# Indirect transfers of a two-layer graph kernel, issued with and without a bound on their indices

## The chip, the cores and the metric

One core of a Trainium2 chip runs the whole kernel. The metric is the device time of one execution in microseconds (us); lower is better. The kernel before was timed three times.

## What is computed

The reference has 8192 nodes with 128 features each and a dense 0/1 adjacency matrix `adj` of 8192 x 8192 with few ones in a row. Two layers, cut to what matters:

```
h = relu(layernorm(x));  H = h @ W.T + b;  s = H @ a_s;  r = H @ a_r
e = leaky_relu(adj * s + adj * r.T);  att = softmax(where(adj > 0, e, -9e15), axis=1)
x = x + att @ H                                     # layer 0
h = relu(layernorm(x)) @ weight
out = relu(adj @ h + bias)
x = x + max over the neighbours j of row i of out[j]   # layer 1
```

## The kernel before, in words

The kernel never multiplies by the whole matrix where it need not. It first turns each row of `adj` into a list of the numbers of its neighbours: tiles of 128 rows stream in by SP's queue, TensorE packs 8 columns into a word (line 862), VectorE finds the words that are not zero with MAX8 (lines 1115 to 1124) and takes them apart. Rows are ordered by their degree, so that the 128 rows of a ranked tile have lists of about one length. There are 63 ranked tiles in four groups (`SLOTS`: 523 list columns in all), and the 128 heaviest rows, the hubs, apart.

GpSimd (POOL) moves everything by those lists. Its program, in order:

- Lines 530 to 540: the table `h_table` (row 0 is a neutral row, row n + 1 is node n) is written from SBUF, 16 direct transfers.
- `rank_group(g)`, four times: each tile of records is scattered to its ranked place (line 547), with direct loads of the next group (525, 527) and of the ranked lists (552).
- `gather_h(q)` (line 563), 63 tiles, 523 transfers: for each list column j one indirect transfer fetches 128 rows of `h_table`, one for each partition, into a slot of `ring`. `ring` has 64 slots; a gather waits on `s_att` until VectorE has used a slot. After each gather, `scatter_y` of the tile five places back (line 576) writes 128 rows of layer 0's result to `y_table`.
- `gather_y(m)` (line 600), 177 transfers, with `scatter_p` (line 608): the sum over neighbours for the light half of the rows. At the same time TensorE multiplies the heavy half by dense bits (line 1010).
- `gather_p(n)` (line 638), 66 tiles, 662 transfers (554 by `srec`, 108 by `seg_slots` for the hubs), with `store_out` (line 645): the maximum over neighbours. VectorE reduces each tile with a tree (line 1225, waits for the gather), adds the input (line 1444), and in between does the rounds that list the hubs' neighbours (lines 1399 to 1412).

A missing neighbour has index 0, the neutral row. No index is beyond its table. The kernel before gives each indirect transfer `bounds_check`, the largest index that may occur. The three gathers also say `oob_is_err=False` (a row with a larger index would be skipped); the four scatters leave that argument at its default, `True`.

```
ring[:, A_AT[q] + j, :], None, h_table,
bass.IndirectOffsetOnAxis(srec_u[g][:, i, LIST + j:LIST + j + 1], 0),
bounds_check=N, oob_is_err=False).then_inc(s_rows[q % BUFS], 16)
```

Counted in the code: 63 + 523 + 63 + 177 + 32 + 662 + 63 = 1583 indirect transfers, all issued by GpSimd.

Of the kernel before, what the change touches and what calls it, by code (L numbers as in the profile page):

```python
# [9 lines left out]
P = 128  # L10
N = 8192
D = 128
# [31 lines left out]
S, RS, OWN, OFF, LEN, ROW, ROW1, OWN1, LIST = range(9)  # L44
# [14 lines left out]
BUFS = 4  # L59
RECORDS = 8  # L60
RESULTS = 8
# [3 lines left out]
def ring_plan(slots, size):  # L65

    first, at = [], 0
    for k in slots:
        if at % size + k > size:
            at += size - at % size  # L70
        first.append(at)
        at += k
    return [a % size for a in first], [sum(b < a + k - size for b in first) for a, k in zip(first, slots)]
# [26 lines left out]
C_AT, C_LEFT = ring_plan(C_SLOTS, RING)  # L100
# [22 lines left out]
def segment_tile(n):  # L123

    return n - HUB_AT if HUB_AT <= n < HUB_AT + HUB_TILES else None


def ranked_tile(n):

    return n if n < HUB_AT else n - HUB_TILES  # L130
# [13 lines left out]
def build(nc, x, adj, W0, b0, a_s, a_r, W1, b1, out):  # L144
    ctx = ExitStack()
    with ctx:
        def sb(name, shape, dt=F32):
            return ctx.enter_context(nc.sbuf_tensor(name, shape, dt))
# [4 lines left out]
        def sem(name):  # L153
            return ctx.enter_context(nc.semaphore(name))
# [3 lines left out]
        p_table = nc.dram_tensor("p_table", [N + 1, D], F32).ap()  # L158
# [11 lines left out]
        ring = sb("ring", [P, RING, D + 1])  # L170
# [8 lines left out]
        rec = [rec_all[:, g % 2, 0:n * (LISTS + LIST + w)].rearrange("p (n c) -> p n c", n=n)  # L179
               for g, (_, n, w) in enumerate(GROUPS)]  # L180
        rec_u = [r.bitcast(U32) for r in rec]
        srec = [sb(f"srec{g}", [P, n, LIST + w]) for g, (_, n, w) in enumerate(GROUPS)]
        srec_u = [r[:].bitcast(U32) for r in srec]
        trec = sb("trec", [P, RECORDS, LISTS])
        results = sb("results", [P, RESULTS, D])
        y_save = rec_all[:, 0, 0:(NR - DENSE_FROM) * D].rearrange("p (m d) -> p m d", d=D)
# [132 lines left out]
        s_onehot, s_counted, s_ranked, s_rec = (sem(n) for n in ("s_onehot", "s_counted", "s_ranked", "s_rec"))  # L319
        s_recin, s_srec = sem("s_recin"), sem("s_srec")  # L320
        s_rows = [sem(f"s_rows{i}") for i in range(BUFS)]
# [5 lines left out]
        s_result = [sem(f"s_result{i}") for i in range(RESULTS)]  # L327
# [3 lines left out]
        s_pscat = [sem(f"s_pscat{i}") for i in range(BUFS)]  # L331
# [174 lines left out]
        def _(pool):  # L506
# [16 lines left out]
            def load_rows(g):  # L523
                a, n, _ = GROUPS[g]
                pool.dma_start(rec[g][:, :, 0:D], x[a * P:(a + n) * P, :].rearrange(
                    "(t p) c -> p t c", p=P)).then_inc(s_recin, 16)
                pool.dma_start(rec[g][:, :, D:LISTS], h_table[a * P + 1:(a + n) * P + 1, :].rearrange(
                    "(t p) c -> p t c", p=P)).then_inc(s_recin, 16)
# [13 lines left out]
            def rank_group(g):  # L542
                _, n, w = GROUPS[g]
                pool.wait_ge(s_recin, 32 * (g + 1))
                pool.wait_ge(s_ranked, g + 1)
                for i in range(n):
                    pool.indirect_dma_start(records[g], bass.IndirectOffsetOnAxis(rank[:, g, i:i + 1], 0),  # L547
                                            rec[g][:, i, :], None, bounds_check=n * P - 1).then_inc(s_rec, 16)
                if g < 3:
                    load_rows(g + 1)  # L550
                pool.wait_ge(s_rec, 16 * sum(m for _, m, _ in GROUPS[:g + 1]))
                pool.dma_start(srec[g][:], records[g][:, LISTS:].rearrange("(t p) c -> p t c", p=P)).then_inc(
                    s_srec, 16)
                pool.wait_ge(s_srec, 16 * (g + 1))

            def gather_h(q):
                g, i, k = RANKED[q]
                if A_LEFT[q] > 0:
                    pool.wait_ge(s_att, A_LEFT[q])
                if q >= BUFS:  # L560
                    pool.wait_ge(s_att, q - BUFS + 1)
                for j in range(k):
                    pool.indirect_dma_start(  # L563
                        ring[:, A_AT[q] + j, :], None, h_table,
                        bass.IndirectOffsetOnAxis(srec_u[g][:, i, LIST + j:LIST + j + 1], 0),
                        bounds_check=N, oob_is_err=False).then_inc(s_rows[q % BUFS], 16)

            def y_row(q):
                return results[:, q % RESULTS, :] if q < DENSE_FROM else y_save[:, q - DENSE_FROM, :]

            def scatter_y(q):
                g, i, _ = RANKED[q]
                pool.wait_ge(s_copied, TURNS[STEP[q] + 3] + 1)
                if q >= RESULTS:
                    pool.wait_ge(s_result[q % RESULTS], 16 * (q // RESULTS))
                pool.indirect_dma_start(y_table, bass.IndirectOffsetOnAxis(srec_u[g][:, i, ROW1:ROW1 + 1], 0),
                                        y_row(q), None, bounds_check=N).then_inc(s_result[q % RESULTS], 16)

            for q in range(NR):
                if RANKED[q][1] == 0:  # L580
                    rank_group(RANKED[q][0])
                gather_h(q)
                if q >= LAG:
                    scatter_y(q - LAG)
            for q in range(NR - LAG, NR):
                scatter_y(q)
# [6 lines left out]
            def gather_y(m):  # L593
                g, i, k = RANKED[DENSE_FROM + m]
                if Y_LEFT[m] > 0:
                    pool.wait_ge(s_ysum, Y_LEFT[m])
                if m >= BUFS:
                    pool.wait_ge(s_ysum, m - BUFS + 1)
                for j in range(k):
                    pool.indirect_dma_start(  # L600
                        ring[:, Y_AT[m] + j, 0:D], None, y_table,
                        bass.IndirectOffsetOnAxis(srec_u[g][:, i, LIST + j:LIST + j + 1], 0),
                        bounds_check=N, oob_is_err=False).then_inc(s_rows[m % BUFS], 16)

            def scatter_p(m):
                g, i, _ = RANKED[DENSE_FROM + m]
                pool.wait_ge(s_ysum, m + 1)
                pool.indirect_dma_start(p_table, bass.IndirectOffsetOnAxis(srec_u[g][:, i, ROW1:ROW1 + 1], 0),  # L608
                                        y_save[:, m, :], None, bounds_check=N).then_inc(s_pscat[m % BUFS], 16)

            for m in range(len(Y_SLOTS)):
                gather_y(m)
                if m >= 3:
                    scatter_p(m - 3)
            for m in range(len(Y_SLOTS) - 3, len(Y_SLOTS)):
                scatter_p(m)
# [7 lines left out]
            def gather_p(n):  # L624
                k = C_SLOTS[n]
                if C_LEFT[n] > 0:
                    pool.wait_ge(s_max, C_LEFT[n])
                if n >= BUFS:
                    pool.wait_ge(s_max, n - BUFS + 1)
                for j in range(k):  # L630
                    if segment_tile(n) is not None:
                        slot = seg_slots[:, segment_tile(n), j:j + 1]
                    else:
                        q = ranked_tile(n)
                        g, i, _ = RANKED[q]
                        column = LIST + j if j < A_SLOTS[q] else OWN1
                        slot = srec_u[g][:, i, column:column + 1]
                    pool.indirect_dma_start(  # L638
                        ring[:, C_AT[n] + j, 0:D], None, p_table, bass.IndirectOffsetOnAxis(slot, 0),
                        bounds_check=N, oob_is_err=False).then_inc(s_rows[n % BUFS], 16)  # L640

            def store_out(n):
                g, i, _ = RANKED[ranked_tile(n)]
                pool.wait_ge(s_max, n + 1)
                pool.indirect_dma_start(out, bass.IndirectOffsetOnAxis(srec_u[g][:, i, ROW:ROW + 1], 0),  # L645
                                        results[:, n % RESULTS, :], None, bounds_check=N - 1).then_inc(
                                            s_result[n % RESULTS], 16)

            for n in range(NC):
                if n == HUB_AT:  # L650
                    pool.wait_ge(s_segin, 16)
                gather_p(n)
                if n >= 3 and segment_tile(n - 3) is None:
                    store_out(n - 3)
            for n in range(NC - 3, NC):
                store_out(n)
# [872 lines left out]
```

## Time and profile before

| | |
|---|---|
| median of 3 runs | 3168.51 us (3162.12 to 3172.34) |
| the profiled execution, its own time | 3148.13 us |
| its span | 3146.3 us |
| POOL busy | 1666.1 us (53%), 1628 instructions |
| VectorE busy | 1667.3 us (53%) |
| TensorE busy | 921.0 us (29%) |
| indirect transfers, line 638, p_table by srec | 567.4 us in 554 |
| indirect transfers, line 563, h_table | 547.5 us in 523 |

A POOL row of a transfer is the time in which GpSimd makes its descriptors, not the time in which the bytes move. POOLq is GpSimd's sequencer: register moves and waits stand under it and are not counted as busy. "Idle before" is the engine's gap before an instruction, with what ended it; "issue" there means that nothing in the profile was waited for.

### The profile page before, as it was taken

What the parts mean: (1) busy time and instruction counts of PE and PEld (TensorE: products, weight loads), DVE (VectorE), ACT (ScalarE), POOL (GpSimd) and SP (SyncE); (2) the same over time, 40 slices, a digit from 0 to 9 for tenths busy, and PEclk for the clock granted to TensorE, in tenths of its full rate; (3) what the DMA queues carried; (4) which work ended last, traced back from release to release, by engine and by line L of the source; (5) the groups of instructions that cost most, each with busy time, mean ns of one, the idle gap of its engine ahead of it and who ended that gap; (6) DMA issues with size and microseconds to landing.
All of it is one profiled execution on the core that took longest, in us unless ns stands there. A gap on an engine that the chain in (4) does not pass through costs nothing.

```text
span 3146.3 us, 19516 instructions
## 1 busy us (share of the span) xinstructions
PE 921.0 (29%) x3633; PEld 419.3 (13%) x3633; DVE 1667.3 (53%) x4416; ACT 377.8 (12%) x769; POOL 1666.1 (53%) x1628
## 2 busy tenths in 40 slices
PE   4785232334323440130017969900000000000000
PEld 1442111111101110120003424400000000000000
DVE  6658878888565686553462535446961431102111
ACT  2331012222000123342330000000000000000000
POOL 0011522333556656755655564366536777667676
PEclk8667666676666775565558979955555555555555
DMA  9679866578857875353222222151203111222121
GB/s 357 234 267 421 248 246 237 208 282 304 253 224 282 314 272 158 67 140 73 72 72 49 69 49 60 39 122 51 58 24 41 49 52 48 46 47 51 43 49 45
DMA packets 121044, 450.31 MB, mean 143 GB/s; under 512 B 31666, under 2 KB 69636, under 8 KB 112596
## 3 DMA queue, kind: packets, MB, share of 16 engines
q1 hardware_dynamic: 42676, 304.96, 24.8%
q0 software_dynamic: 55488, 123.23, 17.3%
q10 hardware_dynamic: 22752, 20.82, 2.1%
q14 instruction: 97, 0.79, 0.1%
q8 instruction: 31, 0.51, 0.1%
HBM read 409.76 MB, written 39.12 MB: 143 GB/s over the span
## 4 chain that ended last, share of the span: by engine, by line
DVE 23%; issue 21%; POOL 17%; PE 16%; DVEq 13%; POOLq 4%; DMA 3%; ACT 2%; SPq 1%; ACTq 0%
POOL ring L638 14%; PE psV L1010 11%; DVE ring L1225 3%; POOLq L638 3%; DVE a_buf L1399 2%; DVE words L1124 2%; DVE words L1115 2%; DVE words L1119 2%; DVEq L1123 2%; DVEq L1118 2%; DVEq L1403 2%; PE psV L862 2%; DVEq L1237 2%; DVE found L1148 1%; DVEq L1147 1%
## 5 line engine op out<-in xcount | busy, mean ns | idle before, releaser
L563 POOL DMA_INDIRECT ring<-h_table,srec x523 | 547.5, 1047 | 501.8 <-DVEq L1247 289.1
L638 POOL DMA_INDIRECT ring<-p_table,srec x554 | 567.4, 1024 | 228.9 <-issue 179.3
L1225 DVE TENSOR_TENSOR ring<-ring 128x128 f32<-128x128 f32 (+8 forms) x498 | 239.7, 481 | 667.9 <-DMA ring<-p_table,srec 465.9
L862 PE MATMUL psV<-a_buf,bit_ident 128*128 128x512 bf16 x1024 | 350.4, 514 | 253.4 <-DVE V L1117 156.7
L1010 PE MATMUL psV<-rec_all,a_buf 128*128 128x512 bf16 x1008 | 236.1, 387 | 37.6 <-issue 36.9
L600 POOL DMA_INDIRECT ring<-y_table,srec x177 | 179.9, 1016 | 56.1 <-issue 55.8
L1020 PE MATMUL psH<-ones_row,flag_col 128*1 128x1 f32 x2 | 0.2, 163 | 691.8 <-DVEq L1470 691.8
L862 PEld LDWEIGHTS psV<-a_buf,bit_ident 128*128 128x128 bf16 x1024 | 122.3, 123 | 471.2 <-issue 227.2
L923 PE MATMUL psT<-ident,hn 128*128 128x128 f32 x63 | 27.4, 438 | 516.4 <-ACT hn L734 450.3
L1375 DVE TENSOR_SCALAR rec_all<-a_buf 128x512 uint16<-128x512 uint16 x336 | 77.4, 302 | 124.7 <-remote 69.9
L638 POOL DMA_INDIRECT ring<-p_table,seg_slots x108 | 108.0, 1000 | 47.8 <-issue 32.3
L1010 PE MATMUL psV<-wbuf,a_buf 128*128 128x512 bf16 x528 | 123.2, 390 | 30.0 <-DVE wbuf L1375 22.4
L532 POOL DMA_DIRECT2D h_table<-stage x16 | 12.3, 767 | 211.9 <-ACT rs_col L689 211.9
L1010 PEld LDWEIGHTS psV<-rec_all,a_buf 128*128 128x128 bf16 x1008 | 97.8, 97 | 169.4 <-issue 53.8
L1115 DVE MAX8 words<-psV 128x8 f32<-128x1024 f32 x63 | 77.7, 1233 | 50.3 <-PE psV L871 32.7
L645 POOL DMA_INDIRECT out<-results,srec x63 | 66.4, 1054 | 70.5 <-DVEq L1445 44.8
L547 POOL DMA_INDIRECT records<-rec_all,rank x63 | 63.2, 1003 | 72.4 <-DVEq L1201 53.5
L608 POOL DMA_INDIRECT p_table<-rec_all,srec x32 | 33.8, 1057 | 121.7 <-DVEq L1364 116.6
L1020 PEld LDWEIGHTS psH<-ones_row,flag_col 128*1 128x1 f32 x2 | 0.1, 80 | 692.0 <-issue 692.0
L1124 DVE MAX8 words<-V 128x8 f32<-128x1024 f32 x65 | 79.8, 1228 | 9.9 <-issue 5.5
L1399 DVE MAX8 a_buf<-V 128x8 f32<-128x1024 f32 x60 | 73.7, 1228 | 20.8 <-issue 16.8
L923 PEld LDWEIGHTS psT<-ident,hn 128*128 128x128 f32 x63 | 11.7, 186 | 535.5 <-issue 532.9
(221 smaller groups left out, 2095.1 us busy)
## 6 DMA issues: line engine op xcount, KB each, us to landing
a_buf<-in_adj SPq DMA_DIRECT2D x64, 4096.0 KB
ring<-p_table,srec POOLq DMA_INDIRECT x554
ring<-h_table,srec POOLq DMA_INDIRECT x523
packed<-wbuf ACTq DMA_DIRECT2D x32, 256.0 KB
a_buf<-packed SPq DMA_DIRECT2D x8, 1024.0 KB
trec<-records ACTq DMA_DIRECT2D x63, 128.5 KB
h_table<-stage POOLq DMA_DIRECT2D x16, 258.0 KB, 6.1
a_buf<-r_row SPq DMA_DIRECT2D x1, 4096.0 KB
```

The lines of the kernel that those rows point to most:

```text
L547: pool.indirect_dma_start(records[g], bass.IndirectOffsetOnAxis(rank[:, g, i:i + 1], 0), rec[g][:, i, :], None, bounds_check=n * P - 1).th ...
L563: pool.indirect_dma_start(ring[:, A_AT[q] + j, :], None, h_table, bass.IndirectOffsetOnAxis(srec_u[g][:, i, LIST + j:LIST + j + 1], 0), bo ...
L600: pool.indirect_dma_start(ring[:, Y_AT[m] + j, 0:D], None, y_table, bass.IndirectOffsetOnAxis(srec_u[g][:, i, LIST + j:LIST + j + 1], 0), ...
L638: pool.indirect_dma_start(ring[:, C_AT[n] + j, 0:D], None, p_table, bass.IndirectOffsetOnAxis(slot, 0), bounds_check=N, oob_is_err=False). ...
L645: pool.indirect_dma_start(out, bass.IndirectOffsetOnAxis(srec_u[g][:, i, ROW:ROW + 1], 0), results[:, n % RESULTS, :], None, bounds_check= ...
L862: last = pe.matmul(psV[n % 2][:, h * BANK:(h + 1) * BANK].rearrange("p (g n) -> p g n", n=P), bit_ident[:, k, :], rows[:, :, k, :], start= ...
L1010: last = pe.matmul(psA[c % 2], y_part[i][:, at:at + D], bit_rows[(c * BLOCKS + b) % 3][:, k, :], start=(b == 0 and k == 0 and i == 0), sto ...
L1115: dve.max(words[:, 0:8], src)
L1124: dve.max(words[:, r:r + 8], V[:])
L1225: dve.tensor_tensor(ring[:, at:at + h, 0:D], ring[:, at:at + h, 0:D], ring[:, at + n - h:at + n, 0:D], op)
L1375: last = dve.tensor_scalar(bit_rows[n % 3][:, k, :].bitcast(U16).rearrange("p (u n) -> p u n", n=P), words_in[c % 2][:, :, b * P:(b + 1) * ...
L1399: dve.max(best, V[:])
```

## The change

All seven kinds of indirect transfer lose their `bounds_check`, and the three gathers lose `oob_is_err=False` with it. The sizes, the order of the instructions, the semaphores and the tables stay.

```diff
                     pool.indirect_dma_start(records[g], bass.IndirectOffsetOnAxis(rank[:, g, i:i + 1], 0),
-                                            rec[g][:, i, :], None, bounds_check=n * P - 1).then_inc(s_rec, 16)
+                                            rec[g][:, i, :], None).then_inc(s_rec, 16)
...
                     pool.indirect_dma_start(
                         ring[:, A_AT[q] + j, :], None, h_table,
-                        bass.IndirectOffsetOnAxis(srec_u[g][:, i, LIST + j:LIST + j + 1], 0),
-                        bounds_check=N, oob_is_err=False).then_inc(s_rows[q % BUFS], 16)
+                        bass.IndirectOffsetOnAxis(srec_u[g][:, i, LIST + j:LIST + j + 1], 0)).then_inc(s_rows[q % BUFS], 16)
...
                 pool.indirect_dma_start(y_table, bass.IndirectOffsetOnAxis(srec_u[g][:, i, ROW1:ROW1 + 1], 0),
-                                        y_row(q), None, bounds_check=N).then_inc(s_result[q % RESULTS], 16)
+                                        y_row(q), None).then_inc(s_result[q % RESULTS], 16)
```

Lines 600 and 638 change as line 563 does, lines 608 and 645 as line 576 does.

In the built program a bound is held in a register. So before the change each of the 1583 indirect transfers has a register move ahead of it on GpSimd (1586 moves in all), and the transfer names that register; after it, 3 moves are left and the transfers name none. Where the kernel waits for a semaphore right before such a transfer, the last wait is carried by the move before the change, and by the transfer itself after it. Nothing moves on the other engines.

## Rows read from the trace of the kernel before

**Rows 1.** The page, busy tenths in 40 slices of the span
```profile
DVE  6658878888565686553462535446961431102111
...
POOL 0011522333556656755655564366536777667676
```

**Rows 2.** Busy time by stretch; columns are named in the first row
```profile
core 0: us, PE busy (x) PEld busy (x) DVE busy (x) ACT busy (x) POOL busy (x), PEclk, DMA share, GB/s
230.00:800.00 570.00, 214.56 (x787) 85.19 (x785) 478.54 (x1187) 103.22 (x166) 190.20 (x187) 0.68 0.76 281
800.00:1205.00 405.00, 133.64 (x420) 50.39 (x420) 265.80 (x725) 51.70 (x95) 236.23 (x223) 0.67 0.70 253
1205.00:1645.00 440.00, 64.81 (x305) 51.32 (x305) 232.60 (x692) 142.12 (x302) 278.17 (x264) 0.53 0.38 99
1645.00:2054.00 409.00, 355.91 (x1568) 154.03 (x1568) 177.31 (x693) 9.61 (x16) 205.45 (x201) 0.91 0.21 55
2054.00:2310.00 256.00, 0.00 (x0) 0.00 (x0) 180.74 (x248) 0.00 (x0) 155.34 (x151) 0.50 0.27 69
2310.00:3147.00 837.00, 0.19 (x2) 0.11 (x2) 187.76 (x410) 0.00 (x0) 585.55 (x574) 0.50 0.22 46
```

**Rows 3.** Waits of POOL from 2310 us to the end: total, times, longest
```profile
POOL ring L638 <- DVEq L1445: 60.2, 7, 26.8
```

**Rows 4.** Waits of VectorE, whole span: total, times, longest
```profile
DVE ring L1225 <- DMA ring<-p_table,srec: 465.9, 46, 61.9
```

**Rows 5.** POOL in order of time, two places: start, duration, gap before (none: no bracket)
```profile
321.25 1.25 POOL L527 DMA_DIRECT2D rec_all<-h_table  x1
...
2613.84 1.00 POOL L638 DMA_INDIRECT ring<-p_table,srec  x1 [0.30 <-issue]
2615.14 1.00 POOL L638 DMA_INDIRECT ring<-p_table,srec  x1 [0.30 <-issue]
2616.45 1.04 POOL L645 DMA_INDIRECT out<-results,srec  x1 [0.31 <-issue]
```

**Rows 6.** Line 563 from 351 to 361 us: count, ns min/median/max, starts
```profile
L563 POOLq MOVE  x19: 29/29/29, 351.2 to 360.5; - x19
L563 POOL DMA_INDIRECT ring<-h_table,srec x7: 997/997/1070, 351.9 to 359.9; - x7
```

**Rows 7.** The lines of the transfers, whole span: ns min/median/max of one
```profile
L638 POOL DMA_INDIRECT ring<-p_table,srec x554: 991/997/2623, 2053.2 to 3130.6; - x185
...
L547 POOL DMA_INDIRECT records<-rec_all,rank x63: 973/976/1599, 299.0 to 1458.2; - x63
...
L645 POOL DMA_INDIRECT out<-results,srec x63: 978/1039/1390, 2128.5 to 3136.2; - x63
...
L532 POOL DMA_DIRECT2D h_table<-stage x16: 750/750/981, 80.5 to 227.3; - x16
...
L527 POOL DMA_DIRECT2D rec_all<-h_table x4: 1153/1214/1255, 234.9 to 1230.2; - x4
```

**Rows 8.** Chain of waits, then all engines in order of time, 547 and 203 us
```profile
547.57 0.03 DVEq L1247
...
548.45 1.02 POOL L563 DMA_INDIRECT ring<-h_table,srec  x1 [11.85 <-DVEq L1247]
...
203.54 0.20 ACT L689 ACTIVATE rs_col<-psH 128x4 f32<-128x4 f32 x1
204.03 0.75 POOL L532 DMA_DIRECT2D h_table<-stage  x1 [11.04 <-ACT rs_col L689]
```

**Rows 9.** Waits of POOL on VectorE, 800 to 1205 us, then 1205 to 1645 us
```profile
POOL ring L563 <- DVEq L1247: 102.9, 9, 45.0
...
POOL y_table L576 <- ACT rec_all L748: 42.4, 8, 10.7
POOL y_table L576 <- DVEq L1247: 13.8, 4, 5.6
```

More of the change, by code:

```diff
@@ L601, in gather_y @@
                         ring[:, Y_AT[m] + j, 0:D], None, y_table,
-                        bass.IndirectOffsetOnAxis(srec_u[g][:, i, LIST + j:LIST + j + 1], 0),
-                        bounds_check=N, oob_is_err=False).then_inc(s_rows[m % BUFS], 16)
+                        bass.IndirectOffsetOnAxis(srec_u[g][:, i, LIST + j:LIST + j + 1], 0)).then_inc(s_rows[m % BUFS], 16)
             def scatter_p(m):
@@ L608, in scatter_p @@
                 pool.indirect_dma_start(p_table, bass.IndirectOffsetOnAxis(srec_u[g][:, i, ROW1:ROW1 + 1], 0),
-                                        y_save[:, m, :], None, bounds_check=N).then_inc(s_pscat[m % BUFS], 16)
+                                        y_save[:, m, :], None).then_inc(s_pscat[m % BUFS], 16)
             for m in range(len(Y_SLOTS)):
@@ L638, in gather_p @@
                     pool.indirect_dma_start(
-                        ring[:, C_AT[n] + j, 0:D], None, p_table, bass.IndirectOffsetOnAxis(slot, 0),
-                        bounds_check=N, oob_is_err=False).then_inc(s_rows[n % BUFS], 16)
+                        ring[:, C_AT[n] + j, 0:D], None, p_table, bass.IndirectOffsetOnAxis(slot, 0)).then_inc(s_rows[n % BUFS], 16)
             def store_out(n):
@@ L645, in store_out @@
                 pool.indirect_dma_start(out, bass.IndirectOffsetOnAxis(srec_u[g][:, i, ROW:ROW + 1], 0),
-                                        results[:, n % RESULTS, :], None, bounds_check=N - 1).then_inc(
+                                        results[:, n % RESULTS, :], None).then_inc(
                                             s_result[n % RESULTS], 16)
```

## The prediction

> **What bounds the kernel now.** I read the page's slices first, to see which engine is dense in which stage [rows 1]: VectorE leads in the first third, and in the last third only POOL has work all the time, at 6 or 7 tenths. Six or seven tenths do not look like a bound, so the second look is at the gaps. POOL in order of time [rows 5] shows one shape over and over: an indirect transfer of 1.00 us, 0.30 us of nothing, the next one, a period of 1.30 us. The gap is "issue": nothing is waited for. So POOL is full when busy time plus 0.305 us for each transfer fills the stretch. By stretches [rows 2]:
>
> - 2310 us to the end: 585.6 + 574 x 0.305 = 761 us of 837. POOL's waits for VectorE are 60.2 us more [rows 3]; that is nearly all of it. VectorE has 188 us of work and waits for the gathers, 465.9 us over all of line 1225 [rows 4]. So this stretch is as long as POOL's 574 transfers and those waits.
> - 1205 to 1645 us: 278.2 + 264 x 0.305 = 359 of 440, 0.81.
> - 800 to 1205 us: 236.2 + 223 x 0.305 = 304 of 405, 0.75. Here VectorE still takes the adjacency apart and POOL waits for it, 102.9 us in 9 waits [rows 9].
> - 230 to 800 us: VectorE busy 478.5 of 570, POOL 190. 1645 to 2054 us: TensorE busy 355.9 of 409. 2054 to 2310 us: VectorE busy 180.7 of 256 and its drains. In these three POOL has slack.
>
> What a nanosecond less per transfer is worth: all 574 of the last stretch less the part behind waits (60 of 837, so 0.93), 534; of the 264, 0.8, 211; of the 223, where POOL and VectorE wait for each other by turns, I take half, 112. Together some 850 transfers. The rest, 187 + 201 + 151, are covered by VectorE, TensorE and VectorE; the tightest is the last of them, where POOL's transfers and gaps fill 155.3 + 151 x 0.305 = 201 us of 256, so they could be a quarter dearer before that cover goes.
>
> **The change, part by part.**
>
> 1. *The register moves.* 1583 x 29 ns [rows 6] would be 46 us if they stood in POOL's way. They do not. Between 351.2 and 360.5 us the sequencer did 19 moves, with the transfers between them, so one turn of move and transfer is 9.3 / 18 = 0.52 us, while POOL got through 7 transfers [rows 6]. The sequencer runs ahead until its queue is full and is then paced by POOL's 1.30 us. Taking 29 ns off a turn of 0.52 us beneath one of 1.30 us gives 0. What hides it is POOL's own work; the cover goes only if a transfer costs POOL under 0.52 us.
>
> 2. *The 0.305 us gap.* It is the same before gathers and scatters, and a direct transfer that follows another has none (line 527 stands right behind 525) [rows 5]. Since the sequencer is ahead, the move is not in it. I cost the gap at no change. Bounds: 0.305 us less if it were made by the bound (850 x 0.305 = 259 us less), nothing more. I take 0, because rows 6 shows that the sequencer isn't late.
>
> 3. *The work of one transfer.* No row shows an unbounded indirect transfer. From below: a direct transfer of 512 rows takes 750 ns, one of 2048 rows 1214 ns, so a row costs 0.3 ns and the gather's 997 ns for 128 rows [rows 7] hold 247 ns or more that direct ones lack: fetching the indices, turning them into addresses, and the check. If all of that were the check: 850 x 0.247 = 210 us less. From above: scatters behind gathers, whose bound is of the default kind, take 1039 ns, 42 more than a gather [rows 7]. If that were the kind of the bound, and an unbounded gather behaved like them, 850 x 0.042 = 36 us more. The nearest row is the scatter of records, line 547: indirect, 128 rows, one after the other with none of another sort between, and without the skipping of rows: 976 ns, 21 less than a gather. I take 21 ns: skipping, which only the gathers have, needs a decision for each row, and the unbounded gather makes none. About 0.93 of the transfers are gathers: 850 x 0.93 x 0.021 = 17 us less.
>
> 4. *The waits.* Before, the last wait sits on the move; when it ends, the transfer behind is still to be decoded and handed over. VectorE's drain on line 1247, which releases the gather, ends at 547.60, and POOL starts at 548.45 [rows 8]: 0.85 us. Where the transfer itself waits, a direct one, ACT ends at 203.74 and POOL starts at 204.03 [rows 8]: 0.29 us. The 0.305 us of an indirect transfer remain to it, so I expect about 0.60 us after the change, 0.25 less; between none and 0.56 less. This counts only for a wait at which POOL really stood and only where POOL is on the path: 7 in the last stretch [rows 3], 9 + 8 + 4 between 800 and 1645 [rows 9], of which I take half: 18 x 0.25 = 5 us less, 0 to 10.
> The Trainium skill ("Perfetto Trace Analysis", section DMA Instruction — SWDGE (GPSIMD)) says that such an instruction is decoded, put into a wait queue with its semaphore wait, and that the sequencer then goes on; by that a wait on the transfer hides its decoding. The 0.29 us of the direct transfer agree.
>
> 5. *Bytes and order.* The same rows move; a faster POOL brings the gathers 2% closer together against a DMA share of 0.22 [rows 2]. Nothing.
>
> Sum: 17 + 5 = 22 us less. The profiled execution took 3148.1 us, so 3126 us in a profile like it; the three timed runs had their median at 3168.5, 20 us above, so 3146 us there. I forecast that median. From about 10 us on, 0.3%, a measurement of this kernel can tell a change from none; spread over 850 transfers that is 11 ns each, which is little, and so the sign hangs on a small cost.
>
> **The rivals.**
>
> *A. The check costs nothing that POOL feels* (chance 0.33). It may run on all rows at once, or on a path that is taken anyway with a bound that is never met. For: 997 against 976 may come from gather against scatter and not from skipping; a row of a direct transfer costs only 0.3 ns, so rows are handled many at a time. Then only the waits are left: 5 us less, 3163, within 0.3%.
> The Trainium skill ("DMA: Bandwidth & Descriptors", section Anatomy of one DMA) calls descriptor generation "small, variable", with most of a transfer's fixed cost in its completion; by that page this rival would hold. The trace disagrees for this kernel as to the whole, since POOL's 1.30 us per transfer set the last stretch, but as to the check it shows nothing.
>
> *B. The check is most of what is special about indirect transfers* (chance 0.10). Then up to 247 ns each, half of it 850 x 0.12 = 105 us less, 3064; all of it, 2958. Against: 128 comparisons are little beside fetching 128 indices from as many partitions.
>
> *C. The unbounded gather is dearer* (chance 0.15). With `oob_is_err=False` the gathers leave a mode of their own and join that of the scatters. Place: line 638 after 2310 us. Price: up to 42 ns, 36 us, less 5 for the waits, 31 more: 3199. It decides from 17 ns per gather on (11 for the bound of a measurement and 6 to pay for the waits). For: the 1039 ns. Against: line 547, of the same mode, has 976 ns, so the 1039 look like the cost of changing from gather to scatter, which line 645 does each time.
>
> *D. The bound is still applied*, from the size of the table. The built program names no bound, so I count this with A.
>
> **How the numbers follow.** My forecast, 10 to 60 ns less for a gather (8 to 47 us, with the waits 13 to 52), has 0.42; A 0.33; B 0.10; C 0.15. Faster by over 0.3%: 0.42 + 0.10 - 0.02 for its lower edge = 0.50. Within: A and the lower edges of the forecast and of C, 0.38. Slower: 0.12. The range leaves out B's greater half with a bit of its lesser, and the upper half of C: 3085 to 3182.
>
> **What would show it.** In the profile after: the row of the sequencer's moves on lines 563 and 638 is gone and the 0.30 us gap stays (if it shrinks, step 2 is wrong); the median of line 638 is about 976 (997 would be A, under 900 B, over 1015 C); line 547, which never skipped, stays at 976; after a wait, POOL starts about 0.60 us behind the drain (0.85 would refute step 4); the last stretch is some 15 us shorter, and 1645 to 2054 us is as long as now. The whole argument fails if the stretches before 2054 us get longer although POOL's transfers do not, which I have no row for.

## The result, and the profile after

| | kernel before | the change |
|---|---|---|
| median | 3163.0 us (3155.4 to 3176.0, 10 runs) | 3179.1 us (3172.2 to 3183.7, 10 runs) |
| ratio | | 1.0033, 95% interval 1.0017 to 1.0048 |
| the profiled execution, its own time | 3148.1 us | 3180.2 us |
| its span | 3146.3 us | 3170.0 us |

Slower by 16 us between the medians and by some 10 us by the ratio (0.0033 x 3163), where 22 us faster was forecast. The time is inside the range, the sign is not. Of the two profiled executions the one of before is 15 us under its median and the one of the change is on it, so some 15 us of what stands between the two traces are no work of the change.

From line 566 on the change's own lines are one to three lower than before: 563 gathers for layer 0 as before, 575 scatters y, 599 gathers y, 636 gathers for the last stage, 642 scatters the output; VectorE's 1247 is 1244, its 1445 is 1442.

By line, whole span, ns min/median/max of one, beside [rows 7]:

```profile
L563 POOL DMA_INDIRECT ring<-h_table,srec x523: 938/944/2802, 352.0 to 1634.9; - x175
L636 POOL DMA_INDIRECT ring<-p_table,srec x554: 940/944/2868, 2089.1 to 3147.2; - x185
L547 POOL DMA_INDIRECT records<-rec_all,rank x63: 956/960/1597, 299.6 to 1486.3; - x63
L642 POOL DMA_INDIRECT out<-results,srec x63: 974/987/1889, 2160.5 to 3152.8; - x63
```

Of the 1586 register moves 3 are left. A gather has fallen from 997 to 944 ns, the scatter of the output from 1039 to 987, the scatter of records from 976 to 960. So a transfer costs POOL less than forecast, and the kernel is slower. POOL in order of time in the change shows the gap unchanged:

```profile
559.37 0.94 POOL L563 DMA_INDIRECT ring<-h_table,srec  x1 [0.30 <-issue]
560.62 0.94 POOL L563 DMA_INDIRECT ring<-h_table,srec  x1 [0.30 <-issue]
```

Busy time by stretch in the change, columns as in [rows 2]:

```profile
800.00:1205.00 405.00, 138.51 (x414) 50.87 (x421) 245.39 (x654) 39.72 (x74) 208.46 (x215) 0.66 0.72 256
1645.00:2054.00 409.00, 325.24 (x1406) 143.23 (x1436) 187.96 (x702) 11.10 (x24) 206.91 (x214) 0.87 0.23 58
2310.00:3170.00 860.00, 0.19 (x2) 0.11 (x2) 220.72 (x460) 0.00 (x0) 591.62 (x586) 0.50 0.22 46
```

From 800 to 1205 us VectorE gets through 654 instructions where it got through 725 [rows 2], and POOL through 215 transfers where it was 223. The work there has not grown, it is late. The best ruler for that is the start of the n-th transfer on POOL, since both programs issue the same 1612 in the same order (us from the start of the span, from the two traces):

| transfer | where it stands | before | the change | later by |
|---|---|---|---|---|
| 71 | a gather of layer 0, first group | 394.1 | 392.5 | -1.6 |
| 271 | a gather of layer 0, second group | 932.7 | 937.5 | 4.8 |
| 421 | a scatter of y, near the end of the second group | 1195.7 | 1227.9 | 32.2 |
| 921 | a gather, 34th transfer of the last stage | 2099.2 | 2132.2 | 33.0 |
| 1611 | the last but one | 3134.8 | 3151.4 | 16.6 |
| 1612 | the last | 3136.2 | 3152.8 | 16.6 |

The last stage gives 16 us back, as forecast, and what stands behind it takes nearly all of them away again. POOL's closing drain, first of before, then of the change (ns, start):

```profile
L146 POOLq DRAIN  x1: 7114/7114/7114, 3138.9 to 3138.9; - x1
```

```profile
L146 POOLq DRAIN  x1: 17700/17700/17700, 3152.1 to 3152.1; - x1
```

From the start of the last transfer to the end of the execution it is 12 us before (3136.2 to 3148.1) and 27 us in the change (3152.8 to 3180.2). Of the 15 us more, 7 lie inside the span and 8 outside it: the execution is 1.8 us longer than its span before, and 10.1 to 11.2 us in all ten executions of the change. What the drain waits for is not shown: the last packet of a transfer's data starts at 3155.1 us, 14.7 us before the drain ends. Taken off the two medians, the last transfer would start at some 3151 us before and 3152 us in the change (an estimate, since each kernel's end is read in one profile). At the medians, then, what is lost early and what is won in the last stage about cancel, and the 16 us are those at the end.

Up to 32 us (part of them the good luck of the profile of before) are lost ahead of transfer 421, where POOL stands at waits for VectorE. Waits of POOL from 380 to 1205 us, first of before, then of the change (total, times, longest):

```profile
POOL ring L563 <- DVEq L1247: 277.9, 19, 67.1
```

```profile
POOL ring L563 <- DVEq L1244: 319.2, 17, 76.6
```

41 us more. And VectorE, which POOL waits for, is idle for nothing. Its waits from 800 to 1205 us that the profile puts down to "issue", in the change:

```profile
DVE rec_all L1175 <- issue: 10.5, 1, 10.5
DVE found L1140 <- issue: 10.4, 6, 3.1
DVE found L1145 <- issue: 10.2, 7, 2.5
DVE node L1137 <- issue: 9.9, 6, 2.5
DVE e_sc L1212 <- issue: 9.2, 3, 3.8
```

and in the kernel before:

```profile
DVE node L1140 <- issue: 9.7, 5, 2.5
DVE l_inv L1235 <- issue: 8.9, 3, 4.2
DVE found L1148 <- issue: 8.9, 6, 2.4
DVE found L1143 <- issue: 8.8, 5, 2.4
DVE rec_all L1178 <- issue: 7.0, 1, 7.0
```

The profile finds nothing that these instructions wait for; most of them read what VectorE itself has just written. Over all lines the "issue" time of VectorE in this stretch is 103.7 us before and 130.5 us in the change. I call them **stalls**. They were in the trace that I predicted from, and I had no term for them. Where VectorE stalls many times in a row, in the change around 390 us, its starts lie 1.40 and 2.81 us apart, multiples of 0.70:

```profile
385.71 0.49 DVE L1130 TENSOR_TENSOR node<-words_no,bit_node 128x320 f32<-128x320 int32 x1 [2.02 <-issue]
387.11 0.49 DVE L1134 SCALAR_TENSOR_TENSOR node<-bits,node 128x320 f32<-128x320 int32 x1 [0.91 <-issue]
...
389.92 0.57 DVE L1137 SCALAR_TENSOR_TENSOR node<-node,label 128x320 f32<-128x320 f32 x1 [2.31 <-issue]
```

POOL has them too, late in the kernel. The chain of waits, kernel before, around 2700 us:

```profile
2699.84 0.70 POOLq L638
2700.53 0.45 POOL ring L638
2700.99 0.25 issue
2701.24 0.70 POOLq L638
```

The register move, 29 ns elsewhere [rows 6], takes 0.70 us here: 286 of GpSimd's moves and waits do, all of them after 2586 us. In the change there are none, but from about 2896 us on more than half of its transfers fall into a beat of 1.40 us, twice 0.70, where they could come every 1.25:

```profile
2904.98 1.10 POOL L636 DMA_INDIRECT ring<-p_table,srec  x1 [0.30 <-issue]
2906.38 1.09 POOL L636 DMA_INDIRECT ring<-p_table,srec  x1 [0.30 <-issue]
2907.77 1.10 POOL L636 DMA_INDIRECT ring<-p_table,srec  x1 [0.30 <-issue]
```

### The profile page after: what moved, and what is told of

Read it like the earlier page. It is cut to its first block, busy times and chain, and to the rows that moved or that the text cites. A ratio compares the mean times of both kernels' runs of the same rounds, so it can differ in the third digit from the quotient of the medians.

```text
span 3170.0 us, 17872 instructions
## 1 busy us (share of the span) xinstructions
PE 919.7 (29%) x3572; PEld 423.6 (13%) x3633; DVE 1666.1 (53%) x4416; ACT 377.8 (12%) x769; POOL 1605.9 (51%) x1628
## 4 chain that ended last, share of the span: by engine, by line
DVE 22%; POOL 22%; issue 20%; PE 16%; DVEq 13%; DMA 3%; ACT 2%; SPq 1%; another core or an unknown queue 1%; ACTq 0%; POOLq 0%
POOL ring L636 17%; PE psV L1007 11%; DVE ring L1222 3%; POOL ring L563 2%; DVE a_buf L1396 2%; DVE words L1121 2%; DVE words L1112 2%; DVE words L1116 2%; DVEq L1120 2%; DVEq L1115 2%; DVEq L1400 2%; PE psV L859 2%; DVEq L1234 2%; POOL out L642 1%; DVE found L1145 1%
## 5 line engine op out<-in xcount | busy, mean ns | idle before, releaser
L563 POOL DMA_INDIRECT ring<-h_table,srec x523 | 517.1, 989 | 556.3 <-DVEq L1244 346.9
L636 POOL DMA_INDIRECT ring<-p_table,srec x554 | 554.7, 1001 | 216.9 <-issue 171.2
L599 POOL DMA_INDIRECT ring<-y_table,srec x177 | 171.1, 967 | 56.0 <-issue 56.0
L1372 DVE TENSOR_SCALAR wbuf<-a_buf 128x512 uint16<-128x512 uint16 x176 | 40.0, 300 | 110.2 <-remote 64.3
L1396 DVE MAX8 a_buf<-V 128x8 f32<-128x1024 f32 x60 | 73.7, 1228 | 23.9 <-issue 20.0
L1121 DVE MAX8 words<-V 128x8 f32<-128x1024 f32 x65 | 79.8, 1228 | 8.4 <-issue 3.9
```

The costliest lines, as they stand in the source:

```text
L563: pool.indirect_dma_start(ring[:, A_AT[q] + j, :], None, h_table, bass.IndirectOffsetOnAxis(srec_u[g][:, i, LIST + j:LIST + j + 1], 0)).th ...
L599: pool.indirect_dma_start(ring[:, Y_AT[m] + j, 0:D], None, y_table, bass.IndirectOffsetOnAxis(srec_u[g][:, i, LIST + j:LIST + j + 1], 0)). ...
L636: pool.indirect_dma_start(ring[:, C_AT[n] + j, 0:D], None, p_table, bass.IndirectOffsetOnAxis(slot, 0)).then_inc(s_rows[n % BUFS], 16)
L1121: dve.max(words[:, r:r + 8], V[:])
L1372: last = dve.tensor_scalar(bit_rows[n % 3][:, k, :].bitcast(U16).rearrange("p (u n) -> p u n", n=P), words_in[c % 2][:, :, b * P:(b + 1) * ...
L1396: dve.max(best, V[:])
```

## The experiments

### Taking the change apart, on a chip with stalls

The change does two things: a transfer is cheaper, and no move stands ahead of it, so that waits sit on the transfer. Two theories stood: P, the cheaper transfers do the harm, by what their denser stream does to VectorE; W, the wait on the transfer does it. Four kernels, run on one chip beside the kernel before (3173.4 us there, 13 runs).

**reg_once** has the moves gone and the transfers as before: all bounds stay, but the values (n x 128 - 1, N, N - 1) are put into registers once.

```diff
+            bound = {v: held(pool, v) for v in sorted({n * P - 1 for _, n, _ in GROUPS} | {N, N - 1})}
...
-                        bounds_check=N, oob_is_err=False).then_inc(s_rows[q % BUFS], 16)
+                        bounds_check=bound[N], oob_is_err=False).then_inc(s_rows[q % BUFS], 16)
```

> All bounds are kept, but each of the four values is put in a register once, so no register move stands ahead of a transfer and the waits sit on the transfers, as after the change. Theory W (the changed kernel's loss between 930 and 1130 us comes with the instruction stream: no moves, waits on the transfers): this kernel shows that loss too, about 30 us more in that stretch, with transfers of 997 ns, so 3185 to 3210 us. Theory P (the loss comes because cheaper transfers shift the gathers against VectorE's steps): gathers of 997 ns, no loss in that stretch, 3155 to 3170 us.

**nop_wait** has the cheap transfers alone: no bounds, and a no-op of the sequencer that carries the wait, where the move stood.

```diff
+                    ahead(pool)
                     pool.indirect_dma_start(
```

> No bounds, but a no-operation of the sequencer stands ahead of each indirect transfer and carries its wait, where the register move stood before. Theory W: gathers of 944 ns and no loss between 930 and 1130 us, so the change's saving shows: 3163 less about 35, 3125 to 3140 us. Theory P: the loss stays, 3170 to 3185 us.

**first_only** takes the bounds from lines 547, 563 and 576 alone, **last_only** from lines 638 and 645 alone (the diff is that of the change, cut to these lines).

> Only the transfers of layer 0 (lines 547, 563, 576) lose their bounds. Both theories: the loss of some 30 us before 1205 us shows here and nothing is won after it, 3180 to 3195 us. If the loss is chance of single executions, 3150 to 3165 us.

> Only the transfers of the last stage (lines 638, 645) lose their bounds. Until 2054 us as before; then 574 transfers at 53 ns less are 30 us less, of which the changed kernel's last 250 us, where the transfers came at 1.40 us each, may take back some 15: 3133 to 3150 us under both theories. If the last stage wins nothing, 3160 us and more.

| | ratio to before | 95% interval | transfer 421 at | transfers 921 to 1611 | last transfer to the end | VectorE's stalls, whole span |
|---|---|---|---|---|---|---|
| before | | | 1195.7 us | 1035.6 us | 12 us | 168 us |
| reg_once (moves gone) | 0.992 | 0.9901 to 0.9939 | 1206.1 | 1022.5 | 21 | 172 |
| last_only | 0.9956 | 0.9939 to 0.9973 | 1208.0 | 1019.4 | 27 | 177 |
| nop_wait (cheap transfers) | 1.007 | 1.0052 to 1.0087 | 1234.4 | 1040.2 | 12 | 213 |
| first_only | 1.0035 | 1.0019 to 1.0052 | 1238.4 | 1037.2 | 12 | 202 |
| the change (both) | 1.0033 | 1.0017 to 1.0048 | 1227.9 | 1019.2 | 27 | 214 |

The last column sums VectorE's idle times over 0.6 us ahead of an instruction that waits for no semaphore. The row of the change is from its own runs, those of the result. The trace of before is of an execution of 3148 us, 25 us under its median beside these kernels, so its 1195.7 us is on the early side.

P gave the direction of reg_once and nop_wait, but both came out past its ranges (3149.1 and 3196.2 us). first_only (3187.4 us) is inside its range; last_only (3162.0 us) is above it. These ranges were worked out from 3163 us for the kernel before; as ratios, nop_wait and last_only stand at the edges of theirs and reg_once stays outside.

What follows: without the moves the kernel gains 25 us (3173.4 x 0.008). In the last stage, where a move can take 0.70 us, the traces show 13 us less, and behind the last transfer 9 us more. The cheaper transfers cost 22 us. The end is longer in the three programs that have neither a move nor a no-op ahead of the transfers of the last stage (21, 27 and 27 us against 12), and longest in the two of them whose last stage has no bounds. The three programs with cheap transfers in layer 0's stage stand apart from the three with bounds there: transfer 421 at 1228 to 1238 us against 1196 to 1208, stalls of 202 to 214 us against 168 to 177. The medians say the same without a trace: first_only is slower than before, last_only faster. The theory that the wait on the transfer itself did the harm has fallen: reg_once has that wait and is the fastest. Single profiles of the same program up to transfer 421 (before and last_only) lie 12 us apart, so the 20 us between the two sets are above that, but not by much.

### The same programs on other chips

The next kernels were made to find what a cheap transfer does to VectorE. They ran on another chip, and there the kernel before takes 2970.4 us.

**reg_mix**: reg_once, with the bounds of the last stage left out. **err_mode**: the kernel before, gathers without `oob_is_err=False`. **nop_first**: the change, with a no-op behind each gather of layer 0. **pace_first**: the change, with a MEMSET there:

```diff
+                    idle_at = sum(x[2] for x in RANKED[:q])
+                    pool.memset(idle[:, idle_at + j:idle_at + j + 1], 0.0)
```

> The bounds of layer 0 and of the y table stay, their values put into registers once; the last stage (p table, out) has no bounds. Theory P (the cheaper transfer does harm only in layer 0's stage, and does good, if anything, in the last): reg_once up to the start of transfer 921 (2106 us), then the last stage of the change (1019 us): 3145 to 3150, ratio 0.991, at or a little below reg_once's 0.992. If the last stage's gain came from the moves alone, it is equal to reg_once; if from the cheaper transfer as well, up to 10 us below (0.989). Rival (what the change loses is one coin thrown by each program, not a matter of the stage): anywhere between 0.992 and 1.007.

> The change, with a MEMSET of one column of an unused tile behind each of the 523 gathers of layer 0. POOL's period there goes from 1.25 to about 1.35 us (a MEMSET of one column takes 0.1 us). By theory P in its form 'pace' (a denser stream of gathers brings the VectorE stalls between 380 and 1205 us earlier and makes them longer) the stalls of VectorE between 800 and 1205 us fall back from 130 to 105 us or less, and transfer 421 starts at 1200 to 1212 us instead of 1230: the kernel at 0.992 to 0.996. By its rival (the loss has nothing to do with pace; the unbounded form itself disturbs, or an offset of VectorE's order against the adjacency's) transfer 421 starts at 1230 or, with a slower POOL, later, and the ratio is 1.003 to 1.010.

> The change, with a sequencer no-op behind each of the 523 gathers of layer 0; waits stay on the transfers. It adds an instruction without adding work to POOL. By 'pace' nothing changes against the change (1.003, transfer 421 at 1230 us, gathers every 1.25 us). If the number of sequencer instructions does the harm, it goes to nop_wait's 1.007 and transfer 421 to 1236 us; if the no-op holds POOL back (period 1.30 or more), it helps as pace_first does.

> The kernel before, all bounds kept, but the gathers without the skipping of rows (the default kind of bound, which the scatters have). It splits the 53 ns by which an unbounded gather is cheaper (944 against 997). Step 3 of the prediction: skipping costs it, so the gather's median is about 944 to 976 and the check itself costs little. Rival: the check of a bound costs it whatever its kind, so the median stays at 997. In time: 1.000 if the median stays; if it falls by half of the 53 ns with the moves kept, up to 1.004.

Measured: reg_mix 0.9859 (0.9844 to 0.9873), pace_first 0.9817 (0.9804 to 0.9829), nop_first 0.9816 (0.9803 to 0.9829), err_mode 1.0032 (1.002 to 1.0044). No expectation on pace was tested: the MEMSET ran inside the gap and slowed nothing, as POOL in order of time in pace_first shows,

```profile
1001.90 0.95 POOL L565 DMA_INDIRECT ring<-h_table,srec  x1 [0.19 <-issue]
1002.85 0.12 POOL L569 MEMSET idle<- 128x1 bf16 x1
1003.15 0.94 POOL L565 DMA_INDIRECT ring<-h_table,srec  x1 [0.19 <-issue]
```

and this chip has no stalls to shorten. err_mode answers its own question, and against both of its expectations. Its gathers took

```profile
L563 POOL DMA_INDIRECT ring<-h_table,srec x523: 1009/1013/3210, 353.1 to 1525.5; - x175
```

1013 ns against 997 with skipping and 944 without a bound: not the skipping costs, the check does, 53 ns with skipping and 69 without.

Theory S was then stated: the stalls belong to the chip, and what the change lost was lost through them. **before_again, after_again, reg_once_again, nop_wait_again** are the four corners once more, unchanged; they ran on a third chip.

> The kernel before once more, for a trace on the same chip as the runs beside it. The second set of runs was on a chip on which this kernel took 2970 us instead of 3163 to 3173, and whose traces have no VectorE stall (idle, nothing waited for) over 1.2 us, where those of the first chip have some 100 to 140 us of them. Theory S (the stalls belong to the chip, not to the kernel): on a chip without them this kernel takes about 2970 us, transfer 921 starts at about 1950 us and no row of VectorE's waits says issue for over 1.2 us; on a chip with them 3165 to 3175 us.

> The change once more. Theory S: what the change loses is lost through the stalls. On a chip without them it is about 53 ns on some 850 to 1000 transfers and the waits faster, so 0.980 to 0.984 of the kernel before (2912 to 2922 us), as nop_first gave (0.982). Rival T (the no-op or MEMSET behind each gather of layer 0 is what made those two fast): 0.99 to 1.003. On a chip with the stalls both say 1.003 again.

> Bounds kept, values in registers once. The share of the moves in the change. Theory S: on a chip without stalls only the waits gain (some 27 in all before 1205 and 2054 to 2310 us included, 0.25 to 0.5 us each, 10 us), 0.995 to 0.998; the rest of the change's gain is the cheaper transfer. On a chip with the stalls 0.992 as before. Rival (the moves themselves cost POOL time everywhere): 0.990 or less.

> No bounds, a no-op ahead of each indirect transfer that carries the wait: only the cheaper transfer is left of the change. Theory S: on a chip without stalls 53 ns times 850 to 1000, 45 to 53 us, 0.982 to 0.985, close to the change. On a chip with the stalls 1.007 as before.

| | ratio to before (2971.5 us, 17 runs) | 95% interval | transfer 421 at | transfer 921 at | transfer 1611 at |
|---|---|---|---|---|---|
| before_again | 0.9998 | 0.9987 to 1.001 | 1139.9 us | 1957.3 us | 2958.5 us |
| reg_once_again (moves gone) | 0.9962 | 0.9948 to 0.9976 | 1135.6 | 1943.7 | 2943.9 |
| nop_wait_again (cheap transfers) | 0.9867 | 0.9849 to 0.9885 | 1133.8 | 1939.5 | 2908.1 |
| after_again (both) | 0.9829 | 0.9814 to 0.9845 | 1139.5 | 1939.8 | 2908.1 |

Theory S's expectations held, but for nop_wait_again's, which had 0.985 as its upper end: the measured 0.9867 is above it, and its interval reaches down to it. Without stalls the moves give 11.3 us, the cheaper transfers 39.5, both together 50.8, which is their sum (closer than the 4 to 5 us to which each is known, so partly by luck). The same instructions take the same time on this chip; before_again's gathers have the 997 ns of [rows 7]:

```profile
L563 POOL DMA_INDIRECT ring<-h_table,srec x523: 992/997/3507, 352.9 to 1528.7; - x175
```

What is gone is the idle time. VectorE's greatest "issue" wait from 800 to 1205 us in before_again, to be read against the rows of before above:

```profile
DVE junk L1150 <- issue: 1.1, 3, 0.5
```

TensorE from 1205 to 2054 us, first before, then before_again (total, times, longest):

```profile
PE psT L923 <- ACT hn L734: 272.8, 21, 48.4
PE psV L1010 <- issue: 44.5, 35, 2.2
PE psF L937 <- issue: 35.9, 6, 14.8
PE psT L923 <- issue: 35.8, 3, 22.9
```

```profile
PE psT L923 <- ACT hn L734: 252.9, 20, 48.3
PE psV L1010 <- DVE wbuf L1375: 22.9, 1, 22.9
PE psF L937 <- ACT hn L762: 19.3, 4, 11.3
PE psF L950 <- ACT hub_n L769: 6.0, 1, 6.0
```

116 us of "issue" on three lines, none among the first four on the other chip. And the chain that ended last, by engine, of before and then of before_again:

```profile
DVE 23%; issue 21%; POOL 17%; PE 16%; DVEq 13%; POOLq 4%; DMA 3%; ACT 2%; SPq 1%; ACTq 0%
```

```profile
POOL 26%; DVE 20%; PE 17%; issue 15%; DVEq 10%; DMA 7%; ACT 3%; SPq 1%; POOLq 1%; ACTq 0%
```

On the chip with stalls 661 us of the chain are "issue", on the other 446 us. That difference of 215 us is more than the 176 us between the two spans, while the busy times are within 1% on VectorE and POOL and 3% on TensorE. So idle time in which nothing is waited for is large enough to make up the whole difference. Theory S goes one step further than the runs: each chip was met in one set of runs only, so whether the stalls belong to the chip or to the hour is not parted. And that the change's loss comes through them rests on where it is absent, and on VectorE's stalls ahead of 1205 us (92 us before, 123 us in the change, measured as in the table above), not on a run that switches them off. Every execution here has a recorded span and clock, so the runs don't tell either whether the stalls are there when nothing is recorded.

### Pace, and the change a third time

Four more, made for the one thing that was open: what in the change lengthens the stalls. **thin_first** has a MEMSET of 128x256 and a drain behind each gather of layer 0; **reg_mix_again**, **nop_first_again** and **after_third** are as above.

```diff
+                    pool.memset(idle[:], 0.0)
+                    pool.drain()
```

> The change, with a MEMSET of 128x256 and a drain on POOL behind each of the 523 gathers of layer 0: POOL's period there goes from 1.25 to 1.5 us or more (the one-column MEMSET of pace_first hid wholly in the gap and slowed nothing). Theory R (on the chip with stalls a dense stream of transfers brings them on): there VectorE's stalls before 1205 us get shorter by half or more, and the kernel is no slower than the change (1.003) or faster, in spite of 0.25 us more for each of 523 gathers. Rival (the stalls come whatever POOL's pace): they stay, and the slower gathers add 223 x 0.25 = 56 us and more, 1.02 or above. On a chip without stalls both say slower than the change: between 0.983 (all hidden) and 1.01 (0.25 us on half of the 523).

> Bounds from registers set once for layer 0 and y, none in the last stage. On the chip with stalls theory P says 0.987 to 0.992, faster than the kernel before, reg_once and the change. On a chip without stalls 0.986 as before, and the change at 0.983 is the better one.

> The change again, on the chip of the two runs beside it: 1.003 on a chip with the stalls, 0.983 on one without. Theory S wants nothing in between unless the traces show stalls of a middling sum.

> The change with a sequencer no-op behind each gather of layer 0. On a chip with the stalls: 1.003 as the change if the stalls hang on POOL's pace, 1.007 and more if they hang on the number of sequencer instructions. On a chip without them 0.982, the same as the change.

They ran on a fourth chip, again without stalls: after_third 0.9823 (0.9806 to 0.984), nop_first_again 0.9821 (0.9807 to 0.9836), reg_mix_again 0.9845 (0.9828 to 0.9862), beside 2968.3 us for the kernel before. thin_first took 4047.8 us, 1.3628: a drain took 2.8 us in the median (2.4 to 10.4), and each of the 523 gathers came (4047.8 - 2916.6) / 523 = 2.16 us dearer. It was meant to add 0.25. It says nothing on stalls, and as a measure of layer 0's slack it is far too coarse. Its expectation missed by a factor of ten because I took the drain for free.

So the cause of the stalls, and whether it is the pace of transfers that lengthens them, stays open. No run that changes the pace alone met a chip that has them.

## Why the prediction was wrong

The shape of the argument held where there are no stalls, which it silently assumed: on two such chips (0.9829, 0.9823) the sign is the forecast one and the size twice it, 51 us for 22. In the measured result, whose traces have the stalls, two things outweigh it that were left out: what the change does to VectorE's stalls (step 5), and what stands behind the last transfer. That the time fell inside the range is luck: it got there on the slower side, by a way that no term described.

- **What bounds the kernel.** Right as far as it went: the last stage is POOL's. Left out: I read "issue" on POOL as the 0.305 us gap and did not ask what "issue" on VectorE and TensorE was. It was the sum that was missing: 103.7 us on VectorE from 800 to 1205 us. Also left out: the end. The forecast has the last stage end with POOL's transfers, but the change needs 27 us from its last transfer to the end where the kernel before needs 12, and these 15 us are about what its last stage wins.
- **Step 1, the moves cost nothing.** Right without stalls as to POOL's pace: transfers come at 997 + 305 ns with the moves and without. Wrong with them: after 2586 us a move can take 0.70 us instead of 29 ns (260 of them do), and reg_once gains 25 us. The 29 ns were read at 351 to 361 us [rows 6] and taken for the whole span. A row from 2700 us would have shown it.
- **Step 2, the gap.** Held: 0.30 us, in every run.
- **Step 3, the transfer.** The direction was right; the mechanism and the size were not. I priced the skipping and took the check for free, and it is the check that costs: 53 ns less for a gather where I took 21, 16 less for line 547 where I took none, 52 less for line 645. The nearest row that I leaned on, 976 ns, is itself bounded, so it could price skipping but not the check. And err_mode shows that skipping costs less than nothing: the default kind takes 16 ns more. The cheaper transfers gave 39.5 us; by 53 ns that is as 745 transfers on the path, where I had counted 850. What I called the cover of the early stages held: up to transfer 421 only 0.4 us was gained (1139.9 against 1139.5; 6.1 us in nop_wait_again).
- **Step 4, the waits.** I kept 0.305 us for the transfer and expected 0.60. In the chain of waits of after_again, at the end of a wait:

```profile
2595.07 0.04 DVEq L1442
2595.11 0.26 issue
2595.37 0.97 POOL ring L636
```

and of before_again, at the same wait:

```profile
2632.08 0.04 DVEq L1445
2632.12 0.02 issue
2632.15 0.03 POOLq L638
2632.18 0.51 issue
2632.68 0.03 POOLq L638
2632.71 0.19 issue
2632.90 0.71 POOL ring L638
```

0.78 us becomes 0.26. The rule that the step quoted from the Trainium skill ("Perfetto Trace Analysis", section DMA Instruction — SWDGE (GPSIMD)), that the sequencer hands the instruction with its wait to a queue and goes on, was the better guide: decoding is hidden whole, as for a direct transfer. Where a second semaphore is waited for in an instruction of its own, 0.83 us became only 0.75. The moves and waits gave 11.3 us for the 5 forecast; 22 waits of 0.52 us would make that.
- **Step 5, bytes and order, "Nothing".** This is the step that failed. With stalls, gathers that come closer together (or are cheaper, the runs do not part the two) went with VectorE's stalls 46 us longer (168 to 214), 32 of them before 1205 us, and from 380 to 1205 us POOL waited 41 us more for VectorE, which is on the path there. That it is the transfers of layer 0 that do it is shown by the runs (first_only and nop_wait have the loss, last_only and reg_once do not); how they do it stays open. The prediction named this as what would sink it, the stretches before 2054 us getting longer, and said that it had no row for it. The trace had one, VectorE's "issue", which I did not read.
- **What would show it.** Moves gone, yes. Gap 0.30, yes. Line 638 at about 976, no: 944. Line 547 unchanged, no: 960. POOL 0.60 us after a release, no: 0.26. Last stretch 15 us shorter: 16.4 by transfers 921 to 1611, yes, but for mixed reasons, and gone again at the end of the execution. Without stalls it is 32.9 us (1001.2 to 968.3), near 574 x 0.053 = 30; with them the beat of 1.40 us takes half of it back.
- **The rivals.** A (the check is free) is refuted by 944 ns, and so are C (dearer) and D (still applied). Yet C's side came true: slower, by a mechanism that none of them named. The rule under A, descriptor generation "small, variable" in the Trainium skill ("DMA: Bandwidth & Descriptors", section Anatomy of one DMA), speaks of the time of one DMA and doesn't carry over to where POOL sets the pace: a gather's descriptors keep POOL for 944 ns even without a bound, and the 53 ns of the bound, 5% of a gather, are 39.5 us of the kernel.

The account for the measured result, from runs with stalls: moves 25 us less, cheaper transfers 22 us more, together 3 us less, and measured 10.5 us more (0.0033 x 3173). Some 14 us are missing. 6 of them lie behind the last transfer, where the change has 15 us more, reg_once 9 and nop_wait none; the other 8 are within what such a sum is known to (three ratios of some 5 us each, 9 us together). On the chip without stalls the end is the same in all (12 us) and the sum closes.

**Which version to use.** Without stalls the change itself, 0.983, with nothing faster among these kernels (nop_first and pace_first are the same within their intervals). With stalls reg_once, 0.992, is faster than the kernel before and the change. reg_mix was made to be good on either; it has 0.986 and 0.985 without stalls and has not been run with them.

## What to carry to other kernels

Sum the "issue" time of every engine on the path, not only of the one that you think is the bound, and take the duration of a cheap sequencer instruction at several places of the span: a 29 ns move that takes 0.70 us elsewhere says that the machine adds something that no instruction of yours explains. Compare what stands behind the last transfer as well: here it undoes what the last stage wins. A change of 1 to 2% can then have either sign, so compare the two versions on more than one chip before you keep or drop it. And price an operation by a row that lacks it: a bounded transfer of another kind says nothing on what the bound costs.

## What the runs showed of the hardware

- The bound of an indirect transfer of 128 rows costs POOL 53 ns in its skipping form (997 against 944) and 69 ns in its default form (1013). If its value is given as a number, a register move of 29 ns stands ahead of each transfer and takes the wait: from release to start 0.78 us instead of 0.26. Put into a register once, it leaves only the 53 ns.
- The 0.305 us between two indirect transfers is open to other POOL work: a MEMSET of 0.12 us ran in it and delayed nothing.
- A drain on POOL behind an indirect transfer and a MEMSET took 2.8 us in the median (2.4 to 10.4, thin_first).
- With stalls the end of the kernel, from the start of the last transfer, took 12 us in programs with a move or a no-op ahead of each transfer of the last stage and 21 to 27 us in those without; without stalls it took 12 us in all. The reason is not shown.
- The same program took 3163 and 3173 us (medians) in the two sets of runs with stalls and 2968 to 2971 us on three other chips, with busy times within 1% on VectorE and POOL and a mean granted clock of 0.627 and 0.636 over the span. The difference lies in stalls of VectorE, TensorE and, late, POOL's sequencer, in which nothing is waited for; where single steps can be read (POOL's moves, VectorE's starts around 390 us) they are of about 0.70 us. On VectorE they sum to 168 to 177 us in programs with bounded gathers in layer 0 and to 202 to 214 us in programs without. What causes them was not found.
